# Attention: VectorE reads TensorE's small results ahead of the column maximum, and two of the events move one step up

## The reference

```python
q, k, v = (x @ Wq.T + bq), (x @ Wk.T + bk), (x @ Wv.T + bv)      # 16 heads of 8
scores  = einsum('bihd,bjhd->bhij', q, k) / sqrt(8)
logits  = li[:, :, None, :] + lj[:, None, :, :] + rel_b           # 3 relations per pair of tokens
bias    = einsum('bijk,hk->bhij', softmax(logits), logical_bias)
scores += sigmoid(x @ gate_W.T + gate_b)[..., None] * bias
out     = einsum('bhij,bjhd->bihd', softmax(scores), v) @ Wo.T + bo
```

## Time and profile before

| | |
|---|---|
| median of 3 runs | 3665.57 us (3654.13 to 3666.7) |
| profiled execution | 3663.69 us, its span 3661.9 us |
| TensorE busy | 3133.4 us, 86% |
| VectorE, ScalarE, GpSimd busy | 2503.8, 2070.3, 2294.0 us |
| granted TensorE clock, mean | 0.951 |

### The profile page before, as it was taken

The page is one execution under the profiler, slowest core; times in us unless marked ns, Lnnn a source line. Parts: engine busy times, 40 slices in busy tenths (PEclk is TensorE's granted clock), DMA queues, the critical chain, the costliest instruction groups (busy, mean ns, idle before and its releaser), DMA issues. The chain is left out here.

```text
span 3661.9 us, 121537 instructions
## 1 busy us (share of the span) xinstructions
PE 3133.4 (86%) x52983; PEld 2292.0 (63%) x52983; DVE 2503.8 (68%) x3404; ACT 2070.3 (57%) x2481; POOL 2294.0 (63%) x1606
## 2 busy tenths in 40 slices
PE   3499999999999999488888888888888888888885
PEld 2377777777777777256666666666666666666664
DVE  5777777777777774366676666766676667666673
ACT  2255555555555554256666666666666666666663
POOL 1545545454554540577777777777777777777772
PEclk7699999999999999699999999999999999999997
DMA  4645454544445450422223222322222232222221
GB/s 110 104 80 88 80 86 78 87 80 86 84 83 85 81 87 5 133 59 57 53 54 90 61 54 65 77 57 61 75 66 54 61 81 63 54 57 60 54 53 38
DMA packets 277481, 260.20 MB, mean 71 GB/s; under 512 B 106263, under 2 KB 220840, under 8 KB 276824
## 3 DMA queue, kind: packets, MB, share of 16 engines
q1 hardware_dynamic: 275272, 252.05, 32.4%
q10 hardware_dynamic: 1680, 0.40, 0.1%
HBM read 98.30 MB, written 40.37 MB: 38 GB/s over the span
## 5 line engine op out<-in xcount | busy, mean ns | idle before, releaser
L660 ACT ACTIVATE prob<-psS 128x1024 f32<-128x1024 f32 x512 | 524.2, 1024 | 603.0 <-PE psS L537 599.9
L824 DVE TENSOR_TENSOR colmax<-psS,colmax 128x1024 f32<-128x1024 f32 x480 | 587.2, 1223 | 315.3 <-PE psS L537 313.5
L537 PE MATMUL psS<-diag,pst 128*128 128x64 bf16 x16384 | 587.3, 195 | 13.9 <-issue 13.7
L537 PEld LDWEIGHTS psS<-diag,pst 128*128 128x128 f16 x16384 | 520.9, 99 | 74.1 <-issue 20.5
L1266 PE MATMUL R<-wqkv,xsT 128*128 128x512 f32 x1152 | 557.4, 607 | 1.5 <-ACT qT L1402 1.1
L529 PE MATMUL psS<-qst,kst 48*128 48x128 bf16 (+1 forms) x8192 | 382.8, 221 | 143.3 <-DMA pst<-p_parts 85.7
L758 POOL TENSOR_TENSOR rel<-rel,rec 128x1024 f32<-128x1024 f32 x64 | 151.8, 2372 | 510.5 <-DVE rec L837 510.5
L1530 POOL TENSOR_TENSOR pr<-pr,rnq 128x1024 f32<-128x1024 f32 x96 | 182.7, 1903 | 394.7 <-DVE pr L1611 394.7
L529 PEld LDWEIGHTS psS<-qst,kst 48*128 48x128 bf16 (+1 forms) x8192 | 235.6, 95 | 301.5 <-issue 156.6
L571 PE MATMUL psO<-prob,v 128*9 128x128 f32 x8192 | 326.3, 276 | 6.0 <-issue 5.4
L1266 PEld LDWEIGHTS R<-wqkv,xsT 128*128 128x128 f32 x1152 | 198.7, 192 | 164.1 <-issue 162.5
(11 more groups left out here) (190 smaller groups left out, 6341.9 us busy)
## 6 DMA issues: line engine op xcount, KB each, us to landing
v<-vs SPq DMA_DIRECT2D x576, 128.0 KB, 2.4
pst<-p_parts SPq DMA_DIRECT2D x512, 128.0 KB, 4.9
p_parts<-stage SPq DMA_DIRECT2D x64, 512.0 KB, 3.0
v<-vs SPq DMA_DIRECT2D x384, 64.0 KB, 2.0
wqkv<-in_L_ffn_Wqkv SPq DMA_DIRECT2D x18, 512.0 KB
q_stack<-qpart SPq DMA_DIRECT2D x6, 512.0 KB
qst<-q_stack SPq DMA_DIRECT2D x32, 96.0 KB, 5.2
wo<-in_L_ffn_Wo SPq DMA_DIRECT2D x6, 512.0 KB
```

The costliest lines, as they stand in the source:

```text
L537: last = pe.matmul(o, pst[:, par, g, P * jb:P * (jb + 1)], diag[:, par, g, h0:h0 + HH // 2, :], start=False, stop=(g == NG - 1), skip_grou ...
L660: act.activation(prob[:, st % 2, :], psS[:, slot_of("b", st)].rearrange("p a b -> p (a b)"), ACT.Exp)\
L824: dve.tensor_tensor(dst, src, dst, ALU.max).then_inc(a_read, 1)
```

## The change

`max1` moves from the end of step 10 to that of step 9, `guard` from the end of step 12 to that of step 11, and ScalarE's issue of the guard's DMAs from behind the exponent of step 13 to behind that of step 12. In each step VectorE now reads the event's result first and takes the column maximum behind it.

```diff
             if not (last and ul == 3):
-                ev[8], ev[10], ev[12] = "max0", "max1", "guard"
+                ev[8], ev[9], ev[11] = "max0", "max1", "guard"
             return ev
...
-                    if jb == 13 and not (last and ul == 3):
-                        guards(events_before(it, ul, 12, first, last) + 1, (ul + 1) % 4)
+                    if jb == 12 and not (last and ul == 3):
+                        guards(events_before(it, ul, 11, first, last) + 1, (ul + 1) % 4)
...
+                    if jb > 0:
+                        take(unit_events(ul, first, last), jb - 1, it, ul, first, last)
                     if not (last and st + LEAD >= 4 * NB):
                         al, ja = divmod(st + LEAD, NB)
                         a_max(b + LEAD, st, al, ja)
-                    if jb > 0:
-                        take(unit_events(ul, first, last), jb - 1, it, ul, first, last)
                     k, o, n, q, r, opens, closes = windows(it, st, last)
```

## The result

The changed kernel takes 3750.54 us (median of 4 runs, 3744.64 to 3769.05) against 3659.85 for the kernel before in the same series (4 runs, 3652.94 to 3666.7): a ratio of 1.0256, 95% interval 1.0213 to 1.0300. The forecast was 3756. The profiled execution has a span of 3749.4 us, 87.5 above that of before; instructions are the same 121,537, and TensorE's busy time grew by 27 us (3133.4 to 3160.1). So the time is waiting, and a slower clock: TensorE's busy time for the same 27 units is 1087.4 us (212 to 1424 us) instead of 1056.8 (212 to 1332), at a mean granted clock of 0.95 instead of 0.99.

What follows compares the result with a forecast made beforehand. TensorE, 86% busy, bounds the kernel, and column maxima have no slack. 15 units at +4.45 and 13 at +1.4 us make 85, taken as 90: 3756 us; range 3652 to 3795.

Steps and rivals of the forecast that it cites:

- L829 earlier wins nothing: Step 9: `largest`, directly behind the maximum, still meets GpSimd's L758 and ends only about 0.13 us before now.
- The chain starts under L509 and is held: Ahead of step 10's maximum, L870, L872 and L874 are held by GpSimd; L870 ends at 453.10.
- held twice: Units whose chain is caught by L509, then L764: 15 of 28, +4.45 us each, 67 us; chance 0.58.
- The second hold by L764: L764 starts at about 453.54 and catches L874 or L873; step 10's maximum comes 4.8 to 5.0 us late.
- That casts are held too: In the chain, L871 and L873 are held by the skill's rule, leaving the delay within 4.8 to 5.0 us.
- The clock's share: Slower clock after TensorE's wait for step 10's maximum: +1.3 us in 15 units, +0.9 in 13.
- The guard's gain: Guard at step 11, issue at 12: saves 0.96 us of wait plus 0.32 of clock, 1.3 per unit.
- issue stalls: Third item among TensorE's stalls in the attention stage: 17 at L537, 0.77 us on average.
- The no-hold rival: Chain's 8-column operations not held: delay 1.4 us against 1.75 given back, 3643 to 3656 us; chance 0.18.

Runs made afterwards that it cites:

- e3: Changed kernel with `largest` (L829) one step later, so GpSimd's L509 starts behind the chain: 3699.14 us, ratio 1.0107.
- e4: Changed kernel with the chain's fp32 intermediate in PSUM instead of SBUF: 3662.42 us, ratio 1.0005.
- e1: Changed kernel with max1, guard and the guard's issue back at steps 10, 12 and 13; reads stay ahead of the maximum: 3751.53 us, ratio 1.0255.
- e5: Kernel before with only the guard's read ahead of the maximum and its DMAs issued behind step 12's exponent instead of 13's: 3649.24 us, ratio 0.9968.
- e7: e5 with one wait added: TensorE's second score group in step 0 waits for step 15's third reciprocal: 3653.95 us, ratio 0.9971.

## Why the prediction was right, point by point

- **L829 earlier wins nothing**: shown. 1.21 us in place of 0.74, its end 2.35 us after the maximum, where L758's end + 0.55 had given 2.34.
- **The chain starts under L509 and is held**: shown in the trace after, by the free chains of the last three units, by e3, where the chain meets no GpSimd instruction, and by e4, where the operand's memory alone takes the price away. The forecast ends were 453.10 for L870, 4.81 us after the maximum of step 9, and 4.8 to 5.0 us of delay; measured are 4.81 (512.93 less 508.12) and, in a unit held twice, 4.98 (7.72 less 2.74). One of the two rows that the forecast named for the hold was no evidence: L1583 lasts 466 to 476 ns in all 96 of its executions, so the 0.47 us under L1517 can't be told from its own length. L829 was.
- **The second hold by L764**: shown. I had put L764 at 453.54, together with L873. In five units it starts about 0.01 us ahead of L873 and catches it; in five it starts at the same time or up to 0.18 us behind it and catches L874. I counted on 15 units, it was 10; the other 18 came out at 5.29 to 5.77 us from maximum to maximum, forecast 5.75.
- **That casts are held too** is shown by L873 (2.14 us) and in e1 by L871 (2.13). The forecast had left this to the Trainium skill ("SBUF — State Buffer", section "Who interferes with whom"), which says that casts can be held where their operands meet certain conditions. L875, a cast from bf16 to fp32 with its columns rearranged, is not held (e4, 178 ns); which condition it misses no run here shows.
- **The clock's share**: steps 11 and 12 hold 129.2 us, of which 87.7 are TensorE's wait and about 6 the guard's transposes (27 x 0.23); some 35 us are left for the slower clock, an estimate. TensorE's busy time, up 30.6 us in this stretch for the same matmuls, says about the same. The forecast had 31 (15 x 1.3 + 13 x 0.9).
- **The guard's gain was mis-sized.** "Gain: 0.96 + 0.32 = 1.3 us per unit", 36 us. The wait does go (23 us at step 0 in the changed kernel), but issue stalls are 12.8 us longer, and in e5, where nothing else changes, 10 of the 27 us won at step 0 are left. The share of the clock in it was also read too high: of the seven stretches at the lower level in 28 units, five stand behind guard waits, and two (from 841.6 and 1271.7 us) behind issue stalls of 1.35 and 2.67 us. The no-hold rival misses too: e4 is that case, and gave 3662 where 3643 to 3656 was forecast.
- The total was right partly by luck. Against the kernel before in the same series the change cost 90.7 us, forecast 90. But five double holds fewer than forecast are worth some 15 us less (5 x (4.45 - 1.4)) and the smaller gain of the guard some 13 more, and these nearly cancel.

## What to carry to other kernels

Before a small VectorE operation is moved, look at what GpSimd does at the new place: with two SBUF inputs (L874), or as a scalar operation or a cast from fp32 to bf16 from SBUF to SBUF (L870, L871, L873), it cost here not its own 0.17 us but the rest of GpSimd's instruction, and a chain of six was caught twice. Put such an intermediate in PSUM, or the chain in a gap of GpSimd. And do not count a removed wait in full: ask which stall behind it the wait was hiding; in this long unrolled program that was probably the fetch of the code.

## What the runs showed that I had not expected

- L875, SBUF to SBUF and 24 columns, runs at 178 ns under L509, while L871 and L873, casts of 8 columns from fp32 to bf16, are held for up to 2.14 us.
- TensorE's issue stalls add up to between 22.5 us (before) and 55.5 us (e3) in 28 units with the same number of TensorE instructions. They grew where the guard's wait was taken away (e5, 42.4) and shrank where a wait was put back (e7, 31.2), but other waits do not order them: e3 waits more than e5 and has the longest.
